# Down products of an expert-choice MoE stage: from full fp32 matmuls to three single passes over split values

## The reference

```python
k = S // E * CAPACITY                       # 256 // 8 * 2 = 64
logits = jnp.einsum('bsd,ed->bse', x, gate_w)
affinity = jnp.transpose(jax.nn.softmax(logits, axis=-1), (0, 2, 1))
gating, idx = jax.lax.top_k(affinity, k)
x_in = x[bidx, idx]
h = jax.nn.silu(jnp.einsum('bekd,eid->beki', x_in, w_gate)) * jnp.einsum('bekd,eid->beki', x_in, w_up)
x_e = jnp.einsum('beki,edi->bekd', h, w_down)
out = jnp.zeros_like(x).at[bidx, idx].add(gating[..., None] * x_e)
...
x = _layernorm(x + ffn(x))
```

## Time and profile before

| what | value |
|---|---|
| time, median of 3 | 2359.95 us (2357.28 to 2373.63) |
| the profiled execution's own time | 2357.93 us |
| its span, first to last instruction | 2356.2 us |
| TensorE busy | 2013.2 us, 85% |
| VectorE, ScalarE, GpSimd busy | 1041.3, 849.0, 649.7 us |
| mean granted TensorE clock, as a share of 2.4 GHz | 0.917 |
| expert loop, first down phase to the end of the last | 685.6 to 960.3 us |

### The profile page before, as it was taken

The page is one execution under the profiler, slowest core; times in us unless marked ns, Lnnn a source line. Parts: engine busy times, 40 slices in busy tenths (PEclk is TensorE's granted clock), DMA queues, the critical chain, the costliest instruction groups (busy, mean ns, idle before and its releaser), DMA issues. The chain is left out here.

```text
span 2356.2 us, 39785 instructions
## 1 busy us (share of the span) xinstructions
PE 2013.2 (85%) x15304; PEld 1466.6 (62%) x15304; DVE 1041.3 (44%) x2771; ACT 849.0 (36%) x2148; POOL 649.7 (28%) x609
## 2 busy tenths in 40 slices
PE   5888957998389999379999995998599996999995
PEld 4677745664368888257777774665466665666663
DVE  2666654565323232235555554555355653312222
ACT  3655532342123232325555543432233332222222
POOL 1433334662422322223333332111100000412222
PEclk9999987997589999689999998997699997999998
DMA  2000011000523422510000002000400003722223
GB/s 59 11 10 20 15 39 32 10 24 15 187 87 106 143 73 44 183 38 2 11 19 10 10 6 63 10 24 15 133 15 15 28 14 127 279 57 46 46 46 91
DMA packets 100034, 127.49 MB, mean 54 GB/s; under 512 B 8682, under 2 KB 86970, under 8 KB 99818
## 3 DMA queue, kind: packets, MB, share of 16 engines
q1 hardware_dynamic: 86554, 107.17, 13.9%
q0 software_dynamic: 13296, 17.77, 4.4%
HBM read 87.12 MB, written 39.89 MB: 54 GB/s over the span
## 5 line engine op out<-in xcount | busy, mean ns | idle before, releaser
L2035 POOL TENSOR_TENSOR L1a_probs<-L1a_probs,L1a_rinv 128x1024 f32<-128x1024 f32 x64 | 121.2, 1894 | 286.3 <-DVE L1a_rinv L2357 286.3
L2032 POOL TENSOR_TENSOR L0a_probs<-L0a_probs,L0a_rinv 128x256 f32<-128x256 f32 (+1 forms) x128 | 103.1, 826 | 203.5 <-DVE L0a_rinv L2357 203.4
L2349 DVE CUSTOM_DVE_ANT_0 L1a_sbias<-L1a_psS,L1a_bias 128x256 f32<-128x256 f32 x256 | 93.2, 421 | 123.7 <-PE L1a_psS L2166 123.7
L2280 ACT ACTIVATE L1a_probs<-L1a_sbias,L1a_nmx 128x256 f32<-128x256 f32 x256 | 126.5, 498 | 40.0 <-DVE L1a_nmx L2349 40.0
L2783 DVE TENSOR_TENSOR ec_hT<-ec_sg,ec_psU 128x512 f32<-128x512 f32 x64 | 44.0, 688 | 194.5 <-ACT ec_sg L2713 194.5
L3228 DVE TENSOR_TENSOR moe_h<-moe_h,moe_psU 128x512 f32<-128x512 f32 x55 | 37.8, 687 | 194.8 <-PE moe_psU L3047 194.8
L2280 ACT ACTIVATE L0a_probs<-L0a_sbias,L0a_nmx 128x128 f32<-128x128 f32 (+1 forms) x256 | 112.8, 443 | 29.8 <-DVE L0a_nmx L2349 29.8
L2654 PE MATMUL ec_psA<-ec_wd,ec_hT 128*128 128x256 f32 x512 | 112.6, 381 | 5.2 <-DVE ec_hT L2783 5.2
L2998 POOL DMA_INDIRECT moe_sums<-moe_y,moe_xg x39 | 60.8, 1559 | 201.1 <-DVE moe_y L3240 198.1
L2589 POOL DMA_INDIRECT ec_sums<-ec_yk,ec_token_at x32 | 50.4, 1574 | 228.7 <-ACT ec_yk L2721 223.8
L2654 PEld LDWEIGHTS ec_psA<-ec_wd,ec_hT 128*128 128x128 f32 x512 | 96.6, 190 | 20.1 <-DVE ec_hT L2783 7.3
(11 more groups left out here) (486 smaller groups left out, 4725.2 us busy)
## 6 DMA issues: line engine op xcount, KB each, us to landing
ec_wg<-in_L_ffn_w_gate SPq DMA_DIRECT2D x8, 1024.0 KB, 8.7
ec_wu<-in_L_ffn_w_up SPq DMA_DIRECT2D x8, 1024.0 KB, 12.3
ec_wd<-in_L_ffn_w_down SPq DMA_DIRECT2D x8, 1024.0 KB, 5.8
moe_rows<-blank SPq DMA_DIRECT2D x1, 5070.0 KB, 21.2
moe_xg<-moe_rows SPq DMA_DIRECT2D x39, 130.0 KB, 2.1
moe_wts<-in_L_ffn_e_gate SPq DMA_DIRECT2D x8, 512.0 KB
moe_wts<-in_L_ffn_e_up SPq DMA_DIRECT2D x8, 512.0 KB
moe_wts<-in_L_ffn_e_down SPq DMA_DIRECT2D x8, 512.0 KB
```

The source lines that it names most:

```text
L2032: last = pool.tensor_tensor(v, v, bcast(rinv[:, r, :, t], 2, KEYS[t]), ALU.mult)
L2035: last = pool.tensor_tensor(v, v, bcast(rinv[:, r, :, :].rearrange("p h t -> p (h t)"), 2, S), ALU.mult)
L2280: ins = act.activation(probs[:, r, j, at], sbias[:, g % 2, j, at], ACT.Exp, bias=nmx[:, r, j, t:t + 1], scale=-1.0, accum_out=sums[:, r, j ...
L2349: last = dve.tensor_tensor_reduce(out=sbias[:, g % 2, j, at], in0=psS[:, slot + j, at], in1=added, scale=-1.0, scalar=LARGE, op0=ALU.add, ...
```

## The change

The hidden values and the down weights are split like the other factors. DVE writes the product of chunk i to a ring of three plain buffers, ec_h. ACT copies it as fp32r to the high half of ec_hT (`hidden_high`), DVE subtracts to make the rest (`hidden_rest`). ec_hT now has two halves. The down weights get halves of their own, ec_wdt: ACT copies the whole of an expert's ec_wd (`down_high`) in step 3, DVE subtracts (`down_rest`) in step 4. ACT's part of chunk i - 1 comes after Silu of chunk i, DVE's part of chunk i - 1 after the product of chunk i. PE's `down` takes three single passes for each product, 96 matmuls per expert. It no longer waits for all eight chunks at once, but in its first group (s = 0) for each chunk's rest before the chunk is used. The buffer of the result, ec_acc, is now the same as that of x.

```diff
@@ -2460,7 +2460,7 @@
         ctx.callback(sem.close)
 
         xt = sb("x", [P, NT, D])
-        acc = sb("acc", [P, NT, D])
+        acc = xt
         gate = sb("gate", [P, KD, E])
         xT = sb("xT", [P, 4, KD, S])
         aff = sb("aff", [P, TT, B, E])
@@ -2482,7 +2482,9 @@
         wt = sb("wt", [P, 2, 2, KD, I], F32R)
         xs = sb("xs", [P, 2, KD, SL], F32R)
         sg = sb("sg", [P, 2, SL])
-        hT = sb("hT", [P, IC, SL])
+        hidden = sb("h", [P, 3, SL])
+        hT = sb("hT", [P, 2, IC, SL], F32R)
+        wdt = sb("wdt", [P, 2, IC, D], F32R)
         yk = sb("yk", [P, 2, ST, D])
         stats = sb("stats", [P, NT, 6])
         mv = sb("mv", [P, NT, 2])
@@ -2505,7 +2507,9 @@
         rows_loaded = [sem("rows_loaded0"), sem("rows_loaded1")]
         x_turned, x_high, x_rest = sem("x_turned"), sem("x_high"), sem("x_rest")
         w_high, w_rest = sem("w_high"), sem("w_rest")
+        d_high, d_rest = sem("d_high"), sem("d_rest")
         up_ready, silu_ready, h_ready = sem("up_ready"), sem("silu_ready"), sem("h_ready")
+        h_high, h_rest = sem("h_high"), sem("h_rest")
         y_ready, y_taken, y_added = sem("y_ready"), sem("y_taken"), sem("y_added")
         last_added = [sem(f"last_added{s}") for s in range(ST)]
         sums_loaded = [sem(f"sums_loaded{s}") for s in range(ST)]
@@ -2644,15 +2648,17 @@
                     last.then_inc(up_ready, 1)
 
                 def down(e):
-                    pe.wait_ge(h_ready, (e + 1) * IC)
-                    pe.wait_ge(down_loaded[e % 2], 16 * (e // 2 + 1))
+                    pe.wait_ge(d_rest, e + 1)
                     for half in range(2):
                         if e:
                             pe.wait_ge(y_taken, (e - 1) * ST + 2 * half + 2)
                         for s in (2 * half, 2 * half + 1):
                             for i in range(IC):
-                                last = pe.matmul(psA[:, half, s % 2 * D:(s % 2 + 1) * D], hT[:, i, s * P:(s + 1) * P],
-                                                 wd[:, e % 2, i, :], start=(i == 0), stop=(i == IC - 1))
+                                if s == 0:
+                                    pe.wait_ge(h_rest, e * IC + i + 1)
+                                for n, (a, b) in enumerate(((0, 0), (0, 1), (1, 0))):
+                                    last = pe.matmul(psA[:, half, s % 2 * D:(s % 2 + 1) * D], hT[:, a, i, s * P:(s + 1) * P],
+                                                     wdt[:, b, i, :], start=(i + n == 0), stop=(i == IC - 1 and n == 2))
                         last.then_inc(y_ready, 1)
 
                 turn_batch(0)
@@ -2703,6 +2709,20 @@
                     for c in range(KD):
                         act.activation(xs[:, 0, c, :], psX[:, c, :], ACT.Copy).then_inc(x_high, 1)
 
+                def down_high(e):
+
+                    act.wait_ge(down_loaded[e % 2], 16 * (e // 2 + 1))
+                    if e:
+                        act.wait_ge(y_ready, 2 * e)
+                    act.activation(wdt[:, 0, :, :], wd[:, e % 2, :, :], ACT.Copy).then_inc(d_high, 1)
+
+                def hidden_high(e, i):
+
+                    act.wait_ge(h_ready, e * IC + i + 1)
+                    if e:
+                        act.wait_ge(y_ready, 2 * e)
+                    act.activation(hT[:, 0, i, :], hidden[:, (e * IC + i) % 3, :], ACT.Copy).then_inc(h_high, 1)
+
                 weight_high(0)
                 row_high(0)
                 for e in range(E):
@@ -2711,6 +2731,11 @@
                         if e or i >= 2:
                             act.wait_ge(h_ready, e * IC + i - 1)
                         act.activation(sg[:, i % 2, :], psG[:, i % 2, :], ACT.Silu).then_inc(silu_ready, 1)
+                        if i:
+                            hidden_high(e, i - 1)
+                        if i == 3:
+                            down_high(e)
+                    hidden_high(e, IC - 1)
                     if e + 1 < E:
                         row_high(e + 1)
                         weight_high(e + 1)
@@ -2735,6 +2760,14 @@
                         dve.wait_ge(w_high, 2 * e + j + 1)
                         dve.tensor_tensor(wt[:, 1, j, :, :], raw[:, e % 2, :, :], wt[:, 0, j, :, :], ALU.subtract)\
                             .then_inc(w_rest, 1)
+
+                def down_rest(e):
+                    dve.wait_ge(d_high, e + 1)
+                    dve.tensor_tensor(wdt[:, 1, :, :], wd[:, e % 2, :, :], wdt[:, 0, :, :], ALU.subtract).then_inc(d_rest, 1)
+
+                def hidden_rest(e, i):
+                    dve.wait_ge(h_high, e * IC + i + 1)
+                    dve.tensor_tensor(hT[:, 1, i, :], hidden[:, (e * IC + i) % 3, :], hT[:, 0, i, :], ALU.subtract).then_inc(h_rest, 1)
 
                 def row_rest(e):
                     for c in range(KD):
@@ -2780,7 +2813,14 @@
                 for e in range(E):
                     for i in range(IC):
                         dve.wait_ge(silu_ready, e * IC + i + 1)
-                        dve.tensor_tensor(hT[:, i, :], sg[:, i % 2, :], psU[:, i % 2, :], ALU.mult).then_inc(h_ready, 1)
+                        if e or i >= 3:
+                            dve.wait_ge(h_rest, e * IC + i - 2)
+                        dve.tensor_tensor(hidden[:, (e * IC + i) % 3, :], sg[:, i % 2, :], psU[:, i % 2, :], ALU.mult).then_inc(h_ready, 1)
+                        if i:
+                            hidden_rest(e, i - 1)
+                        if i == 4:
+                            down_rest(e)
+                    hidden_rest(e, IC - 1)
                     if e + 1 < E:
                         row_rest(e + 1)
                         weight_rest(e + 1)
```

## The result

The changed kernel takes 2339.34 us, the median of four runs (2335.24 to 2341.82); four runs of the kernel before beside it have a median of 2364.95. The ratio is 0.9889, with a 95% interval of 0.9846 to 0.9932. A second set of runs gave 0.9887 (0.9851 to 0.9924). The sum of the prediction was 23.4 us off a profiled 2357.93; the profiled execution after took 2335.24 us, 22.7 less. So the change is faster by about 1.1%. The median lies 4 us over the forecast of 2335 us and inside its own range of 2329 to 2342. That the profiled execution meets the forecast to 0.3 us is luck: it is the fastest of four that lie 6.6 us apart.

A forecast was written before the change was run, and what follows sets the result against it. TensorE was taken as the bound in the eight experts; 17.7 + 4.9 + 1.2 = 23.8 us, less up to 1, taken as 23.4, off 2357.93 gave 2335 us. Own range 2329 to 2342, 8 in 10 within 2326 to 2350.

The forecast's parts named there:

- The down phase, 17.7 us: Eight experts' down products: 96 passes at 0.120 us, 11.5 us in place of 13.73, gaining 17.7 us in all.
- The row of the attention's output projection: Profile row of line L2056, same form as the new passes, from which 0.120 us a pass was taken.
- Rival 1: Down phase: weight loads don't hide under short passes, 0.2145 us a pass, 2407 us in total; chance 4%.
- The bound from above, 0.126: Slowest pass spacing considered for the down phase, from a window holding 42 records; would gain 13.3 us.
- The wait, 6.1 us: TensorE's wait ahead of the down phase goes: 4.9 us over seven experts, 1.2 us in the last.
- Added work at nothing: Copies on ScalarE and subtractions on VectorE, 6.7 and 7.8 us per expert, hidden at no cost.
- The tail: Result copies, DMA adds and normalization after the last down half move with it, changing nothing.
- the reserve: Up to 1 us taken off the 23.8 us sum, leaving 23.4, should product 5 make TensorE late.
- the 1% line: Whole kernel: 23.6 us, about what measurement cannot tell from none; faster by over 1% got 0.48, within 0.46.
- Rival 4: Stages behind get another clock: ten microseconds more or fewer at half clock give 2340 or 2330 us; 13%.
- rival 2: VectorE late in steps 4 to 6, TensorE losing 0.7 to 1.7 us per expert: 2341 to 2349 us; 15%.

The follow-up runs named there:

- e2: The kernel before, plain fp32 down products, but waiting for hidden values chunk by chunk in the first group: 2361.52 us, ratio 0.9982, stage 373.3 us.
- e5: The kernel before, with ACT and DVE also making all halves into tiles no product reads: 2369.01 us, ratio 1.0011, loop 274.7 us.
- e4: The changed kernel with one more 128x2048 subtraction on VectorE ahead of the down weights' rest: 2356.78 us, ratio 0.9978.
- e1: The changed kernel, but waiting once for all eight chunks' rests ahead of the first down pass: 2364.95 us, ratio 1.0018.
- e3: The changed kernel with one pass of three in the down phase, the two products with a rest left out: 2337.87 us, ratio 0.9863.
- e6: The e1 kernel with 18 spare TensorE passes ahead of its single wait: 2355.35 us, ratio 0.9948.
- e7: The e3 kernel with 32 spare TensorE passes behind each expert's down phase but the last: 2320.50 us, ratio 0.9794.
- e8: The changed kernel with 75 and 22 spare TensorE passes before and after the first turning of rows: 2338.58 us, ratio 0.9873.
- a2_again: The changed kernel itself, unaltered, timed in more rounds: 2339.74 us, ratio 0.9887 to the kernel before.

## Why the prediction was right

- *The down phase, 17.7 us.* 0.1206 us a pass for 0.120, 11.59 us for 11.5: 2.14 x 8 = 17.1 us. Against e2, which has the same waits by chunk, the stage is 17.3 us shorter, which includes the 1.3 us of the third item. The row of the attention's output projection was the right one. Rival 1 falls, and with it, for this kernel, the rule in the list "What overlaps and what doesn't" on the Trainium skill's page "TensorE: Matmul & The Clock Gate", that a load overlaps with matmuls in flight only where the row group differs. Loads and passes of the whole array overlap here, and a pass takes 0.1206 us, not the estimated 214 ns. The bound from above, 0.126, was misread. The run of 48 in that window is complete:

```profile
1202.99 6.00 PE L2056 MATMUL L1a_psF<-L1a_wo,L1a_oT 128*128 128x256 f32 x48
```

By the starts of its single records, only the step from the first to the second is long, 0.22 us; the others are 0.112 to 0.121.

- *The wait, 6.1 us.* 0.78 x 7 + 1.1 = 6.6 measured in the change. The last expert gains 2.93 - 1.36 = 1.57 less the 0.43 that it waits, where 0.4 was worked out. In e2, where the last expert waits for nothing, it is 7.2. The turning matmuls follow one another every 0.109 us, as I took them; but the first pass of the change starts 0.03 us behind the last of them, and the second 0.20 behind the first, so 0.08 us only moves from the one row to the other. Wait and down phase together, from psX to psG, were forecast at 12.36 us and took 12.38, for 15.30 before.
- *A term that I did not have.* The first psG group behind the down phase takes 1.39 us; before and in e2 it takes 1.56 to 1.59. It gives 1.3 us over the seven experts that have one behind them. Nothing delays that group before: by the starts of single records, its first matmul starts 0.03 us behind the last psA record, where psA records are 0.216 apart, and its second 0.42 after that. So the boundary is read too early, the 13.73 us of the down phase lack some 0.18, and a record costs 0.216 and not 0.2145 us. The 1.3 us belong to the fp32 products.
- *Added work at nothing.* Shown by e5. The order on VectorE was the tight place: 0.2 to 0.4 us of slack were worked out, and e4 shows 0.2, with TensorE standing for all that goes beyond.
- *The tail.* From the last pass to the third normalization group are 10.5 us for 10.1 before, and to the stage's end 18.6 for 18.3: 0.3 us that I had at nothing. The second half's first add starts as soon behind the last pass as before (1.1 us), so the 0.3 us arise behind the adds; why was not tried.
- *The total.* 23.4 forecast, 24.5 in the stage. The terms came to 23.8 us before the reserve. The 0.6 us too many in the down phase and the 0.6 us too few in the wait of the first seven experts are the same 0.08 us an expert, on the other side of a boundary, and cancel. On top lie the 1.3 us of the third item, less 0.3 us of the tail; the 0.3 us that then remain were not attributed. The measured 1.1% is just beyond the 1% line on which the forecast lay, and its interval, 0.7 to 1.5%, holds both sides. Rival 4 was right in kind: the stages behind scatter by their clock, in both directions, and by more than the 5 us either way that I priced (last section).
- *What the prediction did not see,* though it did no harm: in rival 2 I priced a wait of TensorE by its length. In e1 a stand of 2.2 us costs 1.5 us more behind it in seven of eight experts, in e3 one of 3.3 us costs 2.7 more behind five of seven. Had the change kept its one wait, it would have gained nothing at all (1.0018, 0.9985 to 1.0050). The waits by chunk are worth more than the 5 us of the old wait; they are what lets the passes pay.

## What to carry to other kernels

An fp32 matmul of 256 columns costs 0.43 us in this kernel, three passes over split halves cost 0.36; this pays where the halves can be made under TensorE's cover, so count the queue places of the added work, not only its sum. When a chain between producer and TensorE becomes longer (here two steps more), let TensorE begin on what is ready and wait piece by piece. Where a change makes TensorE stand for 2 us or more, look at the granted clock behind the stand before you price it, and judge a change of 1% by its stage in the trace, not by the total alone.

## What the runs showed that I had not expected

TensorE that stood 2.2 us (3.0 in the last expert) found its clock lowered in seven of eight experts (psA 13.07 in place of 11.59 us), one that stood 1.8 us in none of eight, one that stood 3.3 us in six of seven: two and a half groups at half speed, 2.7 us, in five, and less in one. The length of the stand alone does not decide it: behind stands of the same length the clock was lowered in some experts and full in others. These runs differ in more than the length, too. In e1 the eight turning matmuls come ahead of the stand, in e4 (1.8 us) a psU group, in e3 the down phase with two short waits in it. How much of the difference is the length's was not tried. Extra matmuls in the stand gave it all back (e6, e7). The Trainium skill, page "TensorE: Matmul & The Clock Gate", section "HAM oscillation — how this bites in real kernels", tells of the same thing, a clock that falls in gaps and costs in the burst behind; the traces agree, and the stands of e1 are shorter than the gaps of its example.

The cross attention L1x, far behind this stage and with the same code in all runs, took 205 to 208 us in eight of the eleven profiles, 199.5 in e1, and 223 and 222 in e5 and e8. Windows over it in e1, a2_again and e5 (columns as above):

```profile
1450.90:1650.40 199.50, 178.72 (x1794) 118.91 (x1794) 107.86 (x229) 74.19 (x149) 34.54 (x52) 0.94 0.10 30
...
1420.00:1627.00 207.00, 186.32 (x1794) 122.17 (x1794) 108.09 (x229) 74.18 (x149) 34.05 (x48) 0.90 0.10 30
...
1445.00:1668.00 223.00, 205.01 (x1794) 133.87 (x1794) 107.04 (x229) 74.19 (x149) 35.53 (x52) 0.81 0.09 27
```

The same 1794 matmuls take 16 us more at a granted clock of 0.81 than at 0.90, and 7 less at 0.94. The stage behind, L1s, scatters as much, from 317.6 us at 0.92 (e4) to 334.8 at 0.87 (e7). Each of the two moves the time by some 0.7%, whatever is changed elsewhere. What decides their clock was not tried.
